# One change to a fused language-model layer: where chunk 15's output product, chunk 1's taps and the experts' casts stand

## The chip, the cores and the metric

The kernel runs on one core of one Trainium2 chip. The core has TensorE (matrix products, which write to PSUM), VectorE, ScalarE and GpSimd for everything else, and SyncE, which only starts transfers here. The engines run side by side, each through its own stream of instructions in order, and wait for one another on semaphores. The metric is the device time of one launch in microseconds (us), smaller being better.

## The reference

The reference computes one layer of a language model on 2 x 2048 tokens of width 192:

- a token embedding (a table of 70 rows, scaled) plus a sine position code;
- a Mamba-2 mixer on the normed stream: an input projection to `z`, `x`, `B`, `C` and `dt`; a causal convolution with 4 taps and a SiLU; a state recurrence for 24 heads of 16 channels with 64 states, `h = exp(dt*A) h + dt x B`, `y = h C + D x`; a gate `y * silu(z)`; an output projection; then an RMS norm and a gated MLP of width 768;
- a mixture of experts: a sigmoid router that picks 2 of 8 experts from 2 of 4 groups, gated experts of width 128, and one shared expert of the same shape.

```
h = tok(x)
h = h + attn(layernorm(h))      # mixer, then + m = MLP(rmsnorm(mixer))
h = h + ffn(layernorm(h))       # sum of two chosen experts + the shared one
```

## The kernel before

**Tiling.** The 2048 positions are cut into 16 chunks of 128 positions (`NC`, `Q`), both batch entries (`NB` = 2) side by side. The recurrence runs in chunked form. Within a chunk, pairwise decays are exponentials of differences of running sums, which a transfer through DRAM (`sums_in_rows`, tile `ri`) and a matrix product (`exponents`, line 1707) lay out, ScalarE exponentiates (`exponentials`, line 782, tile `er`) and VectorE cuts and multiplies (`masks`, line 1193, tile `mr`); `masked` (line 1718) sums them on TensorE into the bank `p_y`. There are 12 such units a chunk (`NR`), 6 for each batch entry. What comes from earlier chunks is read out of a state (`state_read`, line 1809; `from_state`, line 1204), and the state is decayed by GpSimd (`decayed`) and added to (`state_share`, line 1818; `new_state`, line 1219). `skipped_x` (line 1795) adds `D x`; `scanned` (line 1213) makes `y`, GpSimd's `gate` (line 510) multiplies it by `silu(z)`, and `project_out` (line 1831) is the output product, with 3 matrix products for each batch entry.

**Stages.** Each chunk has a pre part (embedding, norm), a front part (projection, convolution, scan operands), a scan, and a back part (output product, RMS norm, MLP called `swiglu`, second norm, router, experts). `run` calls `ramp`, then `body(2, 1, 0)`, which is the first round, then a hardware loop of 13 rounds `body(i+2, i+1, i)`, then `finale(14, 15)`. A round interleaves the pre and front part of one chunk, the scan of the next and the back part of the oldest. In the finale both last chunks are left: the scan of chunk 15 beside the back part of 14, and then, interleaved, the experts of 14 and the back part of 15.

**What sets the order.** No planner: every engine has its own `ramp`, `body` and `finale`, and the order of calls in it is the order in its stream. Waits are written out (`wait_ge` on a semaphore that counts chunks or units).

**PSUM.** There are 8 banks: `p_pair[0..1]`, `p_out[0..1]`, `p_misc`, `p_d0`, `p_d1`, `p_y`. Exponents alternate between `p_d0` and `p_d1`. In the finale, the gate and up products of chunk 14's experts go to the banks that `p_gu_a` lists, and chunk 15's output product goes to `p_misc`, both batch entries in a row, behind `gate_up(1)`; ScalarE's `mixed` and `mixed_norm` and VectorE's `v_low` and `mixed` read it there.

**The weights.** High parts in 16 bit are cast from the 32-bit weights, low parts are the rest. The input columns are done first; the middle ones (`middle_weights`, 1536 columns; high on ScalarE, low on VectorE, line 1049) in the ramp; the experts' ones (`last_weights`, 2312 columns) have their high part cast by GpSimd (line 590) at the end of the ramp, and their low part made by VectorE in four halves (line 1057) within the first `swiglu`.

**The convolution.** ScalarE copies the projected `x` out of PSUM (`convolved_in`) and does the first tap (`first_tap`); VectorE adds the three other taps for each of four groups of channels (`taps(c, m)`, line 1132, three instructions each); ScalarE's `convolved_first` (line 707) and `convolved_rest` (line 716) apply the SiLU and write `xs`, and wait until all the readers of the chunk before are through.

**The pair sums.** `operands` writes the running sums into `lj`, first the high part on ScalarE (line 749), then the low part on VectorE (line 1169), and SyncE sends them.

## Time and profile before

| | us |
|---|---|
| median of 3 runs | 796.21 |
| lowest, highest | 795.14, 796.4 |
| the profiled execution | 796.69 |
| its span, first to last instruction | 794.9 |
| TensorE busy | 757.6 (95%) |
| VectorE busy | 636.5 (80%) |
| ScalarE busy | 546.8 (69%) |
| GpSimd busy | 328.3 (41%) |

The profile is of one execution. A share of busy time is a mean over stages with different limits, so a change in one stage is read from the waits and windows of that stage. The profile's clock column (PEclk) gives the TensorE clock that was granted, as a share of 2.4 GHz.

### The profile page before, as it was taken

To read this page: it belongs to the slowest core of one execution; us is meant where nothing else is said; L and a number is where in the kernel's file an instruction comes from. 1 tells how busy PE (TensorE), PEld (TensorE's weight loads), DVE (VectorE), ACT (ScalarE), POOL (GpSimd) and SP (SyncE) were. 2 spreads that over 40 slices of the span, in tenths; PEclk is the share of its full clock that TensorE was granted. 3 is DMA by queue.
4 is the path that set the end of the run, shared out by engine and by line. 5 is a ranking of instruction groups with operands and counts; after the bars stand their busy time and mean duration, and the time that the engine had idled before them with its cause. 6 is when DMAs were issued, how large, how long until landed. Compare 5 with 4: busy or idle time off the path is not lost.

```text
span 794.9 us, 23059 instructions
## 1 busy us (share of the span) xinstructions
PE 757.6 (95%) x7278; PEld 646.6 (81%) x7278; DVE 636.5 (80%) x1691; ACT 546.8 (69%) x1242; POOL 328.3 (41%) x478
## 2 busy tenths in 40 slices
PE   2679999999999999999999999999999999999897
PEld 1556788988888898888888888888988888888786
DVE  4699987879788787978878797887889788786745
ACT  4975777767777776777767677776767777675533
POOL 5355544433444443344344334434443443442222
PEclk9899999999999999999999999999999999999999
DMA  7420000000000000000000000000000000000000
GB/s 251 155 89 1 12 22 12 9 25 6 15 10 21 10 6 25 3 17 10 21 10 6 25 3 17 10 21 10 6 24 4 17 10 16 14 6 11 2 1 21
DMA packets 14923, 18.93 MB, mean 24 GB/s; under 512 B 4656, under 2 KB 13008, under 8 KB 14448
## 3 DMA queue, kind: packets, MB, share of 16 engines
q1 hardware_dynamic: 13264, 15.25, 6.0%
q0 software_dynamic: 1632, 3.34, 1.7%
q8 instruction: 15, 0.25, 0.1%
q14 instruction: 12, 0.10, 0.0%
HBM read 14.39 MB, written 4.19 MB: 23 GB/s over the span
## 4 chain that ended last, share of the span: by engine, by line
PE 87%; DVE 2%; issue 1%; ACT 1%; POOL 0%; DVEq 0%; POOLq 0%; ACTq 0%
PE bank L1554 40%; PE bank L1934 11%; PE bank L1862 8%; PE bank L1718 6%; PE bank L1707 5%; PE bank L1831 4%; PE bank L1818 3%; PE bank L1809 3%; PE bank L1795 2%; PE bank L1647 1%; PE bank L1652 1%; PE bank L1691 1%; DVE mr L1193 1%; PE bank L1901 0%; PE bank L1902 0%
## 5 line engine op out<-in xcount | busy, mean ns | idle before, releaser
L1193 DVE SCALAR_TENSOR_TENSOR mr<-er,gm 128x512 f32<-128x512 f32 x192 | 125.8, 692 | 4.1 <-ACT er L782 3.7
L782 ACT ACTIVATE er<-bank 128x512 f32<-128x512 f32 x192 | 106.0, 595 | 27.4 <-PE bank L1707 27.1
L1934 PE MATMUL bank<-w2t,w_raw 128*128 128x192 f32 x576 | 112.6, 327 | 0.4 <-DVE w_raw L1362 0.4
L872 ACT ACTIVATE sg<-bank 128x256 f32<-128x256 f32 x144 | 55.1, 382 | 61.8 <-PE bank L1554 50.9
L1132 DVE SCALAR_TENSOR_TENSOR xa<-xr,cw_,xa 128x256 f32<-128x256 f32 x192 | 92.4, 488 | 6.3 <-ACT xa L690 4.7
L1934 PEld LDWEIGHTS bank<-w2t,w_raw 128*128 128x128 f32 x576 | 91.0, 190 | 1.8 <-DVE w_raw L1455 0.7
L1554 PE MATMUL bank<-x_h,wt_lo 128*128 128x256 f16 x288 | 78.5, 273 | 0.0
L1554 PE MATMUL bank<-x_h,w_lo 128*128 128x256 f16 x288 | 78.5, 273 | 0.0
L1554 PE MATMUL bank<-x_l,w_hi 128*128 128x256 f16 x288 | 78.5, 272 | 0.0
L1554 PE MATMUL bank<-x_h,w_hi 128*128 128x256 f16 x288 | 78.4, 272 | 0.0
L1554 PE MATMUL bank<-x_h,wt_hi 128*128 128x256 f16 x288 | 78.4, 272 | 0.0
L1862 PE MATMUL bank<-wd,gt 128*128 128x192 f32 x384 | 74.3, 329 | 1.4 <-DVE gt L1239 1.4
L566 POOL TENSOR_TENSOR w_raw<-w_raw 128x384 f32<-128x384 f32 x64 | 64.0, 1000 | 14.9 <-ACT w_raw L860 8.7
L821 ACT ACTIVATE sg<-bank 128x256 f32<-128x256 f32 x90 | 33.9, 376 | 51.5 <-PE bank L1554 51.5
L1362 DVE TENSOR_TENSOR w_raw<-sg,bank 128x256 f32<-128x256 f32 x144 | 59.9, 416 | 11.7 <-ACT sg L872 10.8
L1707 PE MATMUL bank<-ri,lj 128*128 128x512 f16 x192 | 63.7, 384 | 3.3 <-DMA ri<-sums 1.8
L1862 PEld LDWEIGHTS bank<-wd,gt 128*128 128x128 f32 x384 | 60.9, 190 | 2.6 <-DVE gt L1239 2.0
L1718 PE MATMUL bank<-mr,xd 128*32 128x128 f32 x1536 | 57.0, 283 | 1.6 <-DVE mr L1193 1.6
L503 POOL TENSOR_TENSOR state<-state,ends 128x384 f32<-128x384 f32 x31 | 31.8, 1027 | 64.1 <-PE bank L1569 38.3
L1455 DVE SCALAR_TENSOR_TENSOR w_raw<-bank,cw,w_raw 128x192 f32<-128x192 f32 x128 | 47.5, 413 | 10.4 <-POOL w_raw L566 7.5
L445 POOL TENSOR_SCALAR var<-mv 128x2 f32<-128x2 f32 x32 | 7.2, 225 | 113.1 <-DVE mv L1270 62.7
L1239 DVE TENSOR_TENSOR gt<-sg,bank 128x256 f32<-128x256 f32 x90 | 36.2, 414 | 21.9 <-ACT sg L821 21.9
(239 smaller groups left out, 2197.3 us busy)
## 6 DMA issues: line engine op xcount, KB each, us to landing
out<-w_raw SPq DMA_DIRECT2D x16, 192.0 KB, 2.0
pos<-position SPq DMA_DIRECT2D x16, 96.0 KB, 1.9
ri<-exponent_rows SPq DMA_DIRECT2D x1, 1536.0 KB, 6.4
w_raw<-weights SPq DMA_DIRECT2D x1, 1156.0 KB, 6.0
wt_raw<-weights SPq DMA_DIRECT2D x1, 1156.0 KB, 8.4
sums<-lj SPq DMA_DIRECT2D x16, 64.0 KB, 1.9
w2t<-w SPq DMA_DIRECT2D x1, 864.0 KB, 11.6
w_raw<-weights SPq DMA_DIRECT2D x1, 768.0 KB, 8.1
```

Source lines behind the costliest of these rows:

```text
L566: pool.tensor_tensor(acc[:], acc[:], wt_out[:, e % NWT], ALU.add).then_inc(acc_done, 1)
L782: act.activation(er[:, r % NER], p_d[r % 2][:].rearrange("p (h i) -> p h i", h=HG), ACT.Exp)\
L872: act.activation(sg[:, e % 4, :], src[e][:, 0:NB * Q], ACT.Silu).then_inc(sx_ready, 1)
L1132: ve.scalar_tensor_tensor(xa[:, m], xr[:, m, :, k:k + Q], cw_[:, m, k:k + 1], xa[:, m], ALU.mult, ALU.add)\
L1193: ve.scalar_tensor_tensor(mr[:, r % NMR], er[:, r % NER], 1.0, gm[:, r // NQ, :].unsqueeze(1).to_broadcast([128, HG, Q]), ALU.min, ALU.mult)\
L1362: ve.tensor_tensor(hh[:, e % NHH, :], sg[:, e % 4, :], src[e][:, NB * Q:2 * NB * Q], ALU.mult)\
L1455: ins = ve.scalar_tensor_tensor(acc[:, b], p_ex[e][:, b * D:(b + 1) * D], cw[:, b, e - 1:e], acc[:, b], ALU.mult, ALU.add)
L1554: ins = pe.matmul(out_, a, b, start=(i == 0), stop=(i == len(parts) - 1))
L1707: pe.matmul(p_d[r % 2][:].rearrange("p (h i) -> p h i", h=HG), lj[:, b, f, :], ri[:, of, b, f, :], start=True, stop=True).then_inc(d_done, 1)
L1718: ins = pe.matmul(p_y[row:row + 32, k * Q:(k + 1) * Q], xd[:, b, h, :], mr[:, r % NMR, heads.index(h), :], start=False, stop=(h % 2 == 1), ...
L1862: ins = pe.matmul(dst[:, b * D:(b + 1) * D], gt[:, f, b * Q:(b + 1) * Q], wd[:, f, :], start=(f == 0 and b == 0), stop=(f == NF - 1), skip ...
L1934: ins = pe.matmul(p_ex[e][:, b * D:(b + 1) * D], hh[:, e % NHH, b * Q:(b + 1) * Q], w2t[:, e, :], start=True, stop=True)
```

## The change

The names and semaphores:

- `xs_skipped` is a new semaphore, raised by the last `skipped_x` of a chunk. `convolved_first` and `convolved_rest` wait for it and no longer for the last masked product (`yq_done`). So that it comes early, `second_scan` (called in the ramp) issues its three `skipped_x` together.
- Finale: `project_out(15, 0)` is issued ahead of `turn_x(14)`, `project_out(15, 1)` stays behind `gate_up(1)`. Both go to `p_d1`; `gate_up(3)` goes to `p_misc`. `project_out(15, 0)` waits for all of chunk 15's exponentials, `gate_up(3)` for `t1_ready[1]`, `mlp(1)` also for `hm_ready`.
- Ramp: chunk 1's taps stand one place earlier each in VectorE's stream; `operands(0)` goes ahead of `gates(0, 0)` on ScalarE and ahead of `taps(0, 3)` on VectorE; the first middle weights on ScalarE come behind the first four exponentials and `first_tap(1, 1)`.
- GpSimd's two casts of the experts' high parts leave the end of the ramp and stand in the first round, one behind `mixed(0)`, one behind `gate(1, 0)`.

```diff
--- before.py
+++ after.py
@@ -286,7 +286,7 @@
         m_ready = sem("m_ready")
-        yq_done = sem("yq_done")
+        yq_done, xs_skipped = sem("yq_done"), sem("xs_skipped")
         xw_ready = [sem(f"xw_ready{b}") for b in range(NB)]
@@ -310,7 +310,7 @@
         p_gu = (p_pair[0], p_pair[1], p_d0, p_d1, p_pair[0], p_pair[1], p_y, p_pair[1], p_pair[0])
-        p_gu_a = (p_pair[0], p_pair[1], p_d0, p_d1, p_pair[0], p_pair[1], p_pair[0], p_pair[1], p_pair[0])
+        p_gu_a = (p_pair[0], p_pair[1], p_d0, p_misc, p_pair[0], p_pair[1], p_pair[0], p_pair[1], p_pair[0])
         before_a = (None, None, None, None, 0, 1, 4, 5, 6)
@@ -613,19 +613,21 @@
                 halo(1)
-                last_weights(w_hi, w_raw)
-                last_weights(wt_hi, wt_raw)
 
             def body(p, f, b):
...
                 mixed(b)
+                if not later(b):
+                    last_weights(w_hi, w_raw)
                 if f is not None:
...
                     gate(f, 0)
+                if not later(b):
+                    last_weights(wt_hi, wt_raw)
                 if p is not None:
@@ -703,7 +705,7 @@
                     act.wait_ge(xt_done[1], c)
-                    act.wait_ge(yq_done, c * NR)
+                    act.wait_ge(xs_skipped, c)
                 act.activation(xs[:, 0:2], xa[:, 0:2], ACT.Silu).then_inc(xs_first, 1)
...
             def convolved_rest(c):
@@ -712,7 +714,7 @@
                     act.wait_ge(yi_done[1], c)
-                    act.wait_ge(yq_done, c * NR)
+                    act.wait_ge(xs_skipped, c)
                 act.activation(xs[:, 2:NM], xa[:, 2:NM], ACT.Silu).then_inc(xs_ready, 1)
@@ -915,9 +917,9 @@
                 expert_gate(a, 1, p_gu_a)
-                mixed(b, p_misc)
+                mixed(b, p_d1)
                 expert_gate(a, 2, p_gu_a)
-                mixed_norm(b, p_misc)
+                mixed_norm(b, p_d1)
                 expert_gate(a, 3, p_gu_a)
@@ -959,8 +961,8 @@
                 gates(0, 1)
+                operands(0, p_pair[1])
                 gates(0, 0)
-                operands(0, p_pair[1])
                 convolved_first(0)
@@ -971,10 +973,10 @@
                 on_channels(0)
-                middle_weights(0)
                 exponentials(0, range(4))
...
                 first_tap(1, 1)
+                middle_weights(0)
                 exponentials(0, (4, 5))
@@ -1418,10 +1420,10 @@
                 route_experts(a, None, p_gu_a)
-                v_low(b, p_misc)
+                v_low(b, p_d1)
                 route_weights(a, p_gu_a)
                 hidden(a, 4, p_gu_a)
-                mixed(b, p_misc)
+                mixed(b, p_d1)
                 low_in(b, vl_turned, p_d0[:, 0:NB * Q], v_l, v_lo_ready)
@@ -1483,28 +1485,28 @@
                 pre_split(1, p_pair[0][:, NB * Q:2 * NB * Q])
-                taps(0, 3)
                 ve.wait_ge(setup_p, SETUP_P)
                 operands(0, p_pair[1])
+                taps(0, 3)
                 steps_dt(1, p_pair[0])
...
                 masked_g(0)
+                taps(1, 0)
                 masks(0, range(4))
                 from_state(0, 0)
-                taps(1, 0)
+                taps(1, 1)
                 masks(0, (4, 5))
-                taps(1, 1)
                 new_state(0, 0)
                 scanned(0, 0)
+                taps(1, 2)
                 masks(0, (6, 7))
-                taps(1, 2)
+                taps(1, 3)
                 masks(0, (8, 9))
...
                 scanned(0, 1)
-                taps(1, 3)
                 new_state(0, 1)
@@ -1744,7 +1746,8 @@
             def second_scan(c, p, turn, sums=None):
...
                 pe.wait_ge(y_sum[0], c + 1)
-                skipped_x(1, 0)
+                for k in range(KT):
+                    skipped_x(1, k)
                 masked(c, (6, 7))
@@ -1753,12 +1756,10 @@
                     sums()
-                skipped_x(1, 1)
                 masked(c, (8, 9))
...
                     project_in_x(p, p_d, (2, 3), c)
-                skipped_x(1, 2)
                 masked(c, (10, 11))
...
             def scan_front(c, turned):
@@ -1792,8 +1793,10 @@
             def skipped_x(b, k):
-                pe.matmul(p_y[:, k * Q:(k + 1) * Q], skip[:, k], xs[:, k, b, :], start=(k == 0), stop=False,
-                          skip_group_check=True)
+                ins = pe.matmul(p_y[:, k * Q:(k + 1) * Q], skip[:, k], xs[:, k, b, :], start=(k == 0), stop=False,
+                                skip_group_check=True)
+                if b == NB - 1 and k == KT - 1:
+                    ins.then_inc(xs_skipped, 1)
 
             def state_read(c, b, p):
@@ -1818,8 +1821,8 @@
             def project_out(c, b, dst=p_out[0]):
-                if b == 0 and dst is p_misc:
-                    pe.wait_ge(t1_ready[1], c + 1)
+                if b == 0 and dst is p_d1:
+                    pe.wait_ge(e_ready, c * NR + NR)
                 elif b == 0:
@@ -1985,11 +1988,18 @@
                 swiglu(a, None, b)
-                scan_back(b, None, lambda: turn_x(a, None))
+
+                def turn_beside_output():
+                    project_out(b, 0, p_d1)
+                    turn_x(a, None)
+
+                scan_back(b, None, turn_beside_output)
 
                 def gate_up(e):
...
                         pe.wait_ge(gt_ready, a * NF + NF - 1 + e)
+                    elif e == 3:
+                        pe.wait_ge(t1_ready[1], b + 1)
                     elif before_a[e] is None:
@@ -1999,6 +2009,8 @@
                 def mlp(f):
...
                         pe.wait_ge(hh_ready, a * NX + 3 + f)
+                        if f == 1:
+                            pe.wait_ge(hm_ready, b + 1)
                     else:
@@ -2006,8 +2018,7 @@
                 gate_up(1)
-                project_out(b, 0, p_misc)
-                project_out(b, 1, p_misc)
+                project_out(b, 1, p_d1)
                 gate_up(2)
```

## Rows read from the trace of the kernel before

**Rows 1.** The page, part 4: shares of the chain by engine.

```profile
PE 87%; DVE 2%; issue 1%; ACT 1%; POOL 0%; DVEq 0%; POOLq 0%; ACTq 0%
```

**Rows 2.** Windows by stage: us, busy us (and count) by engine, PEclk, DMA share, GB/s.

```profile
62.00:84.00 22.00, 19.95 (x180) 15.29 (x178) 20.50 (x37) 12.86 (x29) 11.86 (x11) 1.00 0.02 5
...
84.00:735.00 651.00, 650.41 (x6364) 560.65 (x6361) 539.14 (x1461) 467.70 (x1073) 271.35 (x401) 1.00 0.05 13
...
735.00:743.00 8.00, 5.97 (x69) 4.49 (x68) 5.88 (x14) 4.63 (x9) 1.49 (x2) 0.79 0.01 3
```

**Rows 3.** What TensorE waited for, 70 to 84 us: us, times, longest.

```profile
PE bank L1862 <- DVE gt L1239: 1.4, 2, 1.1
```

**Rows 4.** Timeline of TensorE, finale: start, us, engine, line, operation [idle before].

```profile
739.43 0.33 PE L1901 MATMUL bank<-idf,xn 128*128 128x128 f32 x1 [1.99 <-DVE xn L1281]
...
740.34 2.79 PE L1718 MATMUL bank<-mr,xd 128*32 128x128 f32 x48
...
745.51 2.12 PE L1831 MATMUL bank<-wo,y 128*128 128x192 f32 x12
```

**Rows 5.** Timelines of ScalarE, GpSimd and VectorE, finale.

```profile
735.24 2.23 ACT L782 ACTIVATE er<-bank 128x512 f32<-128x512 f32 x4
...
725.93 1.00 POOL L510 TENSOR_TENSOR y<-y,zs 128x384 f32<-128x384 f32 x1 [0.63 <-DVE y L1213]
...
741.77 0.42 DVE L1065 TENSOR_TENSOR x_h<-bank,x_h 64x256 f16<-64x256 f32 x1
```

**Rows 6.** Window of 1 us, columns as in rows 2.

```profile
740.00:741.00 1.00, 1.00 (x17) 0.62 (x19) 1.00 (x3) 0.53 (x2) 0.00 (x0) 0.50 0.00 0
```

**Rows 7.** Chain of waits, last loop round: start, us, what.

```profile
694.24 1.47 PE bank L1718 x48
```

**Rows 8.** Timeline of GpSimd, end of the ramp and first round.

```profile
53.75 1.16 POOL L510 TENSOR_TENSOR y<-y,zs 128x384 f32<-128x384 f32 x1 [3.76 <-DVE y L1213]
...
58.10 2.11 POOL L590 CAST wt_hi<-wt_raw 128x2312 f16<-128x2312 f32 x1
...
64.79 1.17 POOL L516 TENSOR_TENSOR rm<-vv,mhalf 128x2 f32<-128x2 f32 x1
...
71.72 1.00 POOL L510 TENSOR_TENSOR y<-y,zs 128x384 f32<-128x384 f32 x1 [0.63 <-DVE y L1213]
```

**Rows 9.** Timeline of TensorE, ramp.

```profile
34.37 0.60 PE L1707 MATMUL bank<-ri,lj 128*128 128x512 f16 x2 [1.79 <-DMA ri<-sums]
...
56.70 1.25 PE L1647 MATMUL bank<-idf,xs 128*128 128x128 f32 x6 [3.84 <-issue]
```

**Rows 10.** Timeline of VectorE, ramp and first round.

```profile
26.19 1.51 DVE L1132 SCALAR_TENSOR_TENSOR xa<-xr,cw_,xa 128x256 f32<-128x256 f32 x3
...
53.59 2.13 DVE L1132 SCALAR_TENSOR_TENSOR xa<-xr,cw_,xa 128x256 f32<-128x256 f32 x3
...
57.35 1.20 DVE L1180 TENSOR_TENSOR xd<-bank,dt_ 128x384 f32<-128x384 f32 x2 [1.04 <-PE bank L1647]
...
58.47 3.35 DVE L1049 SCALAR_TENSOR_TENSOR w_lo<-w_raw,nrm,w_hi 128x1536 f16<-128x1536 f32 x1
...
64.05 3.73 DVE L1193 SCALAR_TENSOR_TENSOR mr<-er,gm 128x512 f32<-128x512 f32 x5
...
72.78 0.42 DVE L1239 TENSOR_TENSOR gt<-sg,bank 128x256 f32<-128x256 f32 x1 [1.14 <-ACT sg L821]
...
73.72 1.35 DVE L1057 TENSOR_TENSOR w_lo<-w_raw,w_hi 128x1156 f16<-128x1156 f32 x1
```

**Rows 11.** Timeline of ScalarE, end of the ramp.

```profile
55.75 0.63 ACT L716 ACTIVATE xs<-xa 128x512 f32<-128x512 f32 x1 [2.11 <-DVE xa L1132]
...
59.43 0.26 ACT L762 ACTIVATE ends<-bank 128x96 f32<-128x96 f32 x1
```

**Rows 12.** GpSimd's line 492: count, ns min/median/max, first and last start.

```profile
L492 POOL TENSOR_TENSOR xw<-xd,ends x31: 837/842/2351, 31.6 to 715.8; 128x384 f32<-128x384 f32 x31
```

**Rows 13.** VectorE's line 1193, columns as in rows 12.

```profile
L1193 DVE SCALAR_TENSOR_TENSOR mr<-er,gm x192: 674/684/1327, 35.4 to 740.2; 128x512 f32<-128x512 f32 x192
```

## The prediction

> **What bounds the kernel now.** Read the chain of waits first: TensorE carries 87% of it [rows 1]. Then the windows of the stages [rows 2]: between 84 and 735 us TensorE is busy for 650.41 of 651 us. The steady loop is therefore TensorE's own work, and the change must pay elsewhere. It touches three places: the ramp (0 to 62 us), the first round, in which chunk 0's back part runs beside chunk 1's scan (62 to 84 us, VectorE busy for 20.50 of 22 us), and the joint between the last two back parts (735 to 743 us, TensorE busy for 5.97 of 8 us at a granted clock of 0.79). In the first round TensorE waits for VectorE's gated products `gt` twice, 1.4 us in all [rows 3]: there VectorE sets the end.
>
> **The loop.** TensorE issues the same instructions in the same order, `second_scan` being called in the ramp alone. `convolved_first` and `convolved_rest` wait on `xs_skipped` in place of `yq_done`, which both come before. One semaphore increment a chunk is added. Cost 0, because a loop without idle time shows no wait that could go; a bound from both sides is 0.1 us.
>
> **The finale: last chunk's output product.** `project_out(15, 0)` is half of 12 records that take 2.12 us [rows 4], so 1.0 us. It moves from behind `gate_up(1)` to ahead of `turn_x(14)`. Its operands are there: ScalarE's last four exponentials end at 735.24 + 2.23 = 737.47 us, the gate product of batch 0 at 726.93 us [rows 5]. TensorE stands idle for 1.99 us until the transposes of `xn` start at 739.43 us [rows 4], so the product ends at 738.5 us, 0.9 us before anybody wants its engine. Gain 1.0 us, if what follows moves up too. It does: `m_out` comes 1.0 us earlier, and the chain from it (squares, `rm` on GpSimd, `v_t`, `v_low`) is followed by work in VectorE's order, so the later wait of TensorE for the low part moves with it and doesn't grow. The new bank of `gate_up(3)` waits only for `t1_ready[1]`, and `mlp(1)` for `hm_ready`, both long past by the order of the streams.
>
> The second part is the clock. After the 1.99 us of idle the granted clock is 0.50 (1.2 GHz) in 740 to 741 us, and the 48 masked products take 2.79 us, where in the loop the same 48 take 1.47 us [rows 4, 6, 7]. With a product in the gap 0.9 us of idle is left, and I expect 2.4 GHz. Of the 1.3 us VectorE lets through only a part: the router waits for the low part `x_h`, which ends at 742.19 us [rows 5] and which VectorE's masks set, not TensorE. The router starts behind the masked products at 743.1 us, so at most 0.9 us; I take 0.8. The bounds are 0 (the clock falls all the same) and 0.9. Finale: 1.0 + 0.8 = 1.8 us.
>
> **The ramp, before Y.** Call Y the end of `scanned(0, 1)`; it is now at 53.7 us, where GpSimd's gate product starts [rows 8]. At the front, ScalarE and VectorE do chunk 0's pair sums before its last taps, so the transfer of the sums, for which TensorE waits 1.79 us until 34.37 us [rows 9], starts some 1.1 us earlier. But the taps (3 in 1.51 us [rows 10]) end 1.2 us later, and with them the SiLU, the transposes and the exponentials on channels. ScalarE drops the first middle weights ahead of the exponentials and does them after `first_tap(1, 1)`. Together the first exponent leaves at about 34.05, not 34.37 us: gain 0.3 us, bounds -0.5 and +0.8, because one side is a DMA that I cannot time under the other's load. From there to Y VectorE has no gap now, and its work up to Y grows by chunk 1's fourth group of taps: +1.5 us. `taps(1, 0)` goes into the wait for the first exponentials, but then `new_state(0, 0)` has to wait for TensorE's state product, which takes that gain back: each later group has only taken the place of the one before. Y = 53.7 - 0.3 + 1.5 = 54.9 us.
>
> **The ramp, after Y.** Now the three taps stand behind Y (53.59 us, 2.13 us), `convolved_rest(1)` waits 2.11 us for them, and TensorE idles 3.84 us until 56.70 us [rows 9 to 11]. All this goes: the transposes start at Y + 0.1 = 55.0 us, 1.7 us earlier. The next to come late is ScalarE: `gates(1, ...)` waits for GpSimd's gate product (1.1 to 1.2 us after Y [rows 8]), then come its gates, a table load and the copy of `bt`, which from the end of `xs` (56.38) to that of the `ends` (59.69 us) take 3.3 us now, about 0.5 of it for `bc`, which will be done before [rows 11]: 54.9 + 1.1 + 2.7 = 58.7 us, 1.0 us earlier. VectorE's `w_lo` now takes 3.35 us, because GpSimd's second cast runs until 60.21 us [rows 8, 10]; 1156 columns of the like take 1.35 us [rows 10], so its 1536 want 1.7 to 1.8. `masked_g` follows at 58.6 us, then GpSimd's first `weighted_x` (0.84 us [rows 12]), `wt_lo` (1.7 us), the second `weighted_x` (0.84 us), one behind the other, and the first mask of chunk 1. It ends at about 62.8, against 65.4 us now (64.05 and the longest mask, 1.33 us [rows 10, 13]): gain 2.6 us, Y's own delay counted.
>
> **The casts in the first round.** Each is 2.11 us on GpSimd [rows 8]. GpSimd has room for both; the price falls on VectorE. The row is `w_lo`: started at 58.47 us beside a cast with 1.74 us to go, it took 1.6 us more than its columns want. `xw` takes 2351 ns at most against 842 in the middle, a mask 1327 against 684 [rows 12, 13]. So I let an instruction of VectorE that reads two SBUF operands stand still while GpSimd casts, and one with an operand in PSUM run: two `xd` took 1.20 us beside the casts [rows 10]. The Trainium skill has the same in "SBUF — State Buffer", section "Who interferes with whom": a VectorE instruction with two SBUF inputs contends with a GpSimd one that reads SBUF, and the loser is blocked for the whole of the other. That rule speaks against this change, and the trace agrees with it (3.35 us).
>
> The first cast now follows `rm`, which ends at 65.96 us, 6.3 us after the `ends`, 0.4 of it for the second `weighted_x` [rows 8, 11]; changed, 58.7 + 5.9 = 64.6 us. VectorE is then in chunk 1's masks (0.64 us each, two SBUF operands). The cast comes either ahead of mask 4, and costs the whole 2.1 us, or behind it, when `from_state` and `v_low`, with one operand in PSUM each, run beside it, and costs 1.1 us. Mask 4 would start at 62.8 + 3 x 0.64 = 64.7 us, 0.1 us from the cast; I take the middle, 1.6 us. The second cast follows `gate(1, 0)`. Now VectorE's first `w_lo` half of the experts ends at 75.0 us, 2.3 us behind that gate's end at 72.72 us [rows 8, 10]. With 2.11 us of cast between gate and one of mask 6 and `w_lo`, it comes 2.11 + 0.64 + 1.27 = 4.0 us behind it: costs 1.8 us. From there to 84 us VectorE is dense, so nothing of it is made up. Bounds of both casts together: 0 and 4.2 us, with 3.4 taken, near the upper end because the nearest row, `w_lo`, shows the whole overlap as lost.
>
> **The sum.** Ramp and first round: -2.6 + 1.6 + 1.8 = +0.8 us. Finale: -1.8 us. Together -1.0 us. The profiled execution took 796.69 us (span 794.9 and 1.8 around it), so it would take 795.7. The runs' median is 796.21, half a microsecond shorter; the clock's fall in the finale may be a part of that and is then gained in some executions only, so I take 0.8 off the median: 795.4 us.
>
> **Rivals.** First, the casts are hidden after all: the first comes behind mask 4 and the second falls beside `gt` products, of which one operand is in PSUM. Then the sum is -1.8 - 2.6 + 1.1 = -3.3 us, some 793 us; with half of that hidden, -2.2 us. For it: VectorE waits 1.1 us for ScalarE just there [rows 10]. Against it: GpSimd's gate fills that wait already. Chance 0.36 for all that ends more than 1.6 us below. Second, on the other side: TensorE's clock falls in the waits that the change opens. One is new at 29 us (about 0.8 us, for the late taps), another grows in the first round from 1.4 us by the 1.8 us of the second cast. The price of one fall is the finale's, 2.79 - 1.47 = 1.3 us, or up to 1.5 us where more dense work follows; both give +3.0, in sum +2.0 us, 798.2 us. It decides once it costs over 1.0 us, two falls or one that hits dense work; against it, a wait of 1.1 us in the first round now leaves the clock at 1.00 [rows 2, 3]. Chance 0.12 for more than 1.6 us above. Third, the change doesn't do what it says: the product in the finale waits longer than the gap lasts and pushes the transposes. Then the finale gives 0 to 1.0 us and the time is 796.2 to 797; its operands' ends [rows 5] speak against it, and it counts with my forecast's own band, 0.05.
>
> **Numbers.** My forecast, no change that can be told, has 0.52 with the third rival in it; faster 0.36, slower 0.12. A measurement of this kernel tells about 0.2%, 1.6 us, from no change. The range goes from 793.1 (casts hidden) to 797.3 us (one fall of the clock beside the upper costs).
>
> **What would show it.** Right: the output product's 6 records before the `xn` transposes and no 0.50 in the clock around 740 us; the wait before chunk 1's transposes down from 3.84 us to under 1.5; `w_lo` of the middle weights near 1.7 us; one mask of chunk 1 and mask 6 or the first `w_lo` of the experts longer by up to 2 us beside a cast; the loop's length the same to 0.3 us. Wrong: masks at 0.68 us beside the casts (then the first rival), Y below 54 us, or the end of the first round more than 1 us away from +0.8.

## The result, and the profile after

The changed kernel takes 797.29 us (median of 20 runs, 795.37 to 799.14), the kernel before 796.1 us in the same comparison (20 runs, 794.39 to 796.91): ratio 1.0016, 95% interval 1.0010 to 1.0023. It is slower by 1.2 us: 0.16%, inside the 0.2% that the text called no change, but the interval leaves no change out. 795.4 us was forecast. The time lies at the edge of the range (797.3), and the sign is wrong. Four of the 20 runs took 795.37 to 795.75 us, about the forecast's time; of none of them is there a trace. The profiled execution took 797.69 us with a span of 795.9, against 796.69 and 794.9 before, so the two traces differ by the same 1.0 us as is to be explained.

The first view is the windows of the stages of the changed kernel (us, busy us and count by engine, granted clock, DMA share, GB/s); they answer to [rows 2]. In this kernel lines up to 1,100 have moved by 2, those behind by 2 or 3.

```profile
62.00:84.00 22.00, 19.41 (x166) 14.56 (x164) 18.15 (x31) 10.39 (x26) 10.45 (x10) 0.90 0.01 1
84.00:735.00 651.00, 649.34 (x6353) 559.68 (x6353) 541.19 (x1464) 468.57 (x1074) 273.52 (x402) 1.00 0.05 13
735.00:743.00 8.00, 7.21 (x58) 6.00 (x60) 4.78 (x13) 4.06 (x7) 1.49 (x2) 1.00 0.00 1
```

The joint in the finale is as forecast: TensorE busy for 7.21 us in place of 5.97, clock 1.00 in place of 0.79. The first round is not: VectorE, which set the end there, is busy for 18.15 us in place of 20.50, and the clock is 0.90.

The residual sum `h` closes each chunk, so its rows cut the span into stages. VectorE's timeline of `h`, the kernel before, chunks 0, 14 and 15:

```profile
84.24 0.55 DVE L1257 TENSOR_TENSOR h<-bank,hm 128x384 f32<-128x384 f32 x1
...
735.50 0.56 DVE L1257 TENSOR_TENSOR h<-bank,hm 128x384 f32<-128x384 f32 x1 [1.12 <-PE bank L1862]
...
767.67 0.56 DVE L1257 TENSOR_TENSOR h<-bank,hm 128x384 f32<-128x384 f32 x1 [0.56 <-PE bank L1862]
```

The same rows of the changed kernel:

```profile
87.04 0.55 DVE L1259 TENSOR_TENSOR h<-bank,hm 128x384 f32<-128x384 f32 x1
...
738.08 0.56 DVE L1259 TENSOR_TENSOR h<-bank,hm 128x384 f32<-128x384 f32 x1 [1.12 <-PE bank L1865]
...
768.68 0.56 DVE L1259 TENSOR_TENSOR h<-bank,hm 128x384 f32<-128x384 f32 x1 [0.56 <-PE bank L1865]
```

Ramp and first round lost 2.80 us (87.04 - 84.24), the loop gained 0.22 (651.04 against 651.26), the finale gained 1.57 (30.60 against 32.17), and behind the last `h` both take 27.2 us: 2.80 - 0.22 - 1.57 = 1.01 us. The finale was forecast at -1.8, the loop at 0; ramp and first round at +0.8. There lies the miss of 2.0 us.

VectorE's timeline of the changed kernel from Y on (start, us, engine, line, operation, [idle before <- releaser]); it answers to [rows 10]:

```profile
54.23 0.56 DVE L1215 TENSOR_TENSOR y<-bank,t 128x384 f32<-128x384 f32 x1
...
56.39 1.81 DVE L1051 SCALAR_TENSOR_TENSOR w_lo<-w_raw,nrm,w_hi 128x1536 f16<-128x1536 f32 x1
...
58.88 2.31 DVE L1051 SCALAR_TENSOR_TENSOR wt_lo<-wt_raw,nrm,wt_hi 128x1536 f16<-128x1536 f32 x1
61.11 1.92 DVE L1195 SCALAR_TENSOR_TENSOR mr<-er,gm 128x512 f32<-128x512 f32 x2
63.50 0.69 DVE L1195 SCALAR_TENSOR_TENSOR mr<-er,gm 128x512 f32<-128x512 f32 x1 [0.47 <-ACT er L784]
65.39 3.21 DVE L1195 SCALAR_TENSOR_TENSOR mr<-er,gm 128x512 f32<-128x512 f32 x2 [1.19 <-ACT er L784]
68.52 0.54 DVE L1206 TENSOR_TENSOR t<-bank,ecx 128x384 f32<-128x384 f32 x1
...
74.28 0.42 DVE L1241 TENSOR_TENSOR gt<-sg,bank 128x256 f32<-128x256 f32 x1 [1.36 <-ACT sg L823]
74.61 1.98 DVE L1195 SCALAR_TENSOR_TENSOR mr<-er,gm 128x512 f32<-128x512 f32 x1
76.52 1.35 DVE L1059 TENSOR_TENSOR w_lo<-w_raw,w_hi 128x1156 f16<-128x1156 f32 x1
```

TensorE in the same stretch, in answer to [rows 9]:

```profile
54.89 0.85 PE L1649 MATMUL bank<-idf,xs 128*128 128x128 f32 x6 [1.08 <-DVE y L1215]
...
59.45 1.03 PE L1709 MATMUL bank<-ri,lj 128*128 128x512 f16 x2 [2.14 <-DMA ri<-sums]
60.28 2.13 PE L1834 MATMUL bank<-wo,y 128*128 128x192 f32 x6
```

TensorE of the kernel before, the same instructions:

```profile
60.65 0.59 PE L1707 MATMUL bank<-ri,lj 128*128 128x512 f16 x2 [0.57 <-ACT ecx L770]
61.08 1.14 PE L1831 MATMUL bank<-wo,y 128*128 128x192 f32 x6
```

And GpSimd of the changed kernel, in answer to [rows 8]:

```profile
58.74 3.15 POOL L492 TENSOR_TENSOR xw<-xd,ends 128x384 f32<-128x384 f32 x2 [2.71 <-ACT ends L764]
...
65.74 2.31 POOL L590 CAST w_hi<-w_raw 128x2312 f16<-128x2312 f32 x1
...
73.94 2.11 POOL L590 CAST wt_hi<-wt_raw 128x2312 f16<-128x2312 f32 x1
```

Y ends at 54.8 us (54.9 forecast). The 3.84 us wait before chunk 1's transposes is 1.08, and `w_lo` takes 1.81 us in place of 3.35. The masks start at 61.11 us, 2.94 us earlier than before. Up to here the steps held. Then comes what the sum has no term for: VectorE waits 0.47 and 1.19 us for ScalarE's exponentials `er`. TensorE's first two exponents start only 1.20 us earlier than before (59.45 against 60.65). It waited 2.14 us for the transferred pair sums of chunk 1 (before, 0.57 us in this place, and for ScalarE's `ecx`), and then did chunk 0's output product at 1.2 GHz: 2.13 us for six products, against 1.14 before. The fall of the clock is not new but has moved: before, it came behind the wait of 3.84 us, the granted clock was 0.50 in 58 to 60 us and 0.90 in 60 to 62; now it is 0.85 and then 0.50. The first cast stands beside the fifth mask (the pair takes 3.21 us, unhindered 1.29), the second beside the seventh (1.98 against 0.69).

From before to after, VectorE's path to `w_lo` of the experts moves by: masks' start -2.94; waits for `er` +1.66; the five masks' own time +2.09 (5.82 against 3.73); between `t` and the first `gt` +0.69; the seventh mask +1.30. Of the 2.09 us, 1.92 are the held pair's. That is +2.80 us, and `w_lo` starts at 76.52 in place of 73.72 us.

### The profile page after: what moved, and what is told of

It reads as the page before. It is cut to its first block, busy times and chain, and to the rows that moved or that the text cites. A ratio compares the mean times of both kernels' runs of the same rounds, so it can differ in the third digit from the quotient of the medians.

```text
span 795.9 us, 23060 instructions
## 1 busy us (share of the span) xinstructions
PE 755.6 (95%) x7278; PEld 644.3 (81%) x7278; DVE 638.4 (80%) x1691; ACT 546.5 (69%) x1242; POOL 325.8 (41%) x478
## 4 chain that ended last, share of the span: by engine, by line
PE 89%; DVE 4%; issue 3%; ACT 1%; DMA 1%; POOL 1%; DVEq 0%; POOLq 0%; SPq 0%; ACTq 0%
PE bank L1556 40%; PE bank L1937 11%; PE bank L1865 8%; PE bank L1720 6%; PE bank L1709 5%; PE bank L1834 4%; PE bank L1821 3%; PE bank L1812 3%; PE bank L1796 2%; PE bank L1649 1%; DVE mr L1195 1%; PE bank L1654 1%; PE bank L1693 1%; DVE xa L1134 1%; PE bank L1904 0%
## 5 line engine op out<-in xcount | busy, mean ns | idle before, releaser
L1195 DVE SCALAR_TENSOR_TENSOR mr<-er,gm 128x512 f32<-128x512 f32 x192 | 129.2, 709 | 2.0 <-ACT er L784 1.7
L1720 PE MATMUL bank<-mr,xd 128*32 128x128 f32 x1536 | 55.0, 278 | 1.4 <-DVE mr L1195 1.4
L1556 PE MATMUL bank<-v_h,w_hi 128*128 128x256 f16 x192 | 52.6, 274 | 0.8 <-issue 0.8
```

The lines of the kernel that those rows point to most:

```text
L1195: ve.scalar_tensor_tensor(mr[:, r % NMR], er[:, r % NER], 1.0, gm[:, r // NQ, :].unsqueeze(1).to_broadcast([128, HG, Q]), ALU.min, ALU.mult)\
L1556: ins = pe.matmul(out_, a, b, start=(i == 0), stop=(i == len(parts) - 1))
L1720: ins = pe.matmul(p_y[row:row + 32, k * Q:(k + 1) * Q], xd[:, b, h, :], mr[:, r % NMR, heads.index(h), :], start=False, stop=(h % 2 == 1), ...
```

## The experiments

Two theories. **C**: the casts, where they now are, hold VectorE's instructions with two SBUF operands, and that is the loss. **K**: the loss is TensorE's, which waits for the transferred sums and falls to 1.2 GHz. All kernels were timed against the kernel before; h(0) and h(15) are the starts of `h` of chunks 0 and 15 in the profiled execution, in us. They tell of one execution each, which can lie 2 us off its kernel's median. The kernel before ran beside each group again, with medians of 795.79 to 796.08 us, so kernels of different groups are compared by the ratio.

| kernel | median (lowest to highest) | ratio, 95% interval | h(0) | h(15) |
|---|---|---|---|---|
| before | 796.1 | | 84.24 | 767.67 |
| changed | 797.29 (795.37-799.14) | 1.0016, 1.0010-1.0023 | 87.04 | 768.68 |
| e1 finale alone | 794.8 (793.6-795.28) | 0.998, 0.9972-0.9989 | 84.05 | 765.75 |
| e2 casts alone | 797.59 (795.59-799.57) | 1.002, 1.0009-1.0031 | 87.56 | 770.26 |
| e3 changed, both casts back | 794.79 (794.57-795.16) | 0.9987, 0.9979-0.9996 | 84.27 | 765.92 |
| e4 ramp's order alone | 796.04 (795.57-797.53) | 1.0004, 0.9995-1.0013 | 84.18 | 767.40 |
| e5 casts on ScalarE | 795.95 (794.41-796.61) | 0.9996, 0.9988-1.0005 | 83.68 | 766.76 |
| e6 e5 + early sums | 795.9 (794.39-797.09) | 1.0001, 0.9992-1.001 | 82.77 | 765.80 |
| e7 e6 + filler | 795.09 (794.66-796.26) | 0.9994, 0.9985-1.0002 | 83.18 | 766.28 |
| e8 changed + early sums, filler | 794.77 (794.52-798.65) | 1.0008, 0.9994-1.0021 | 83.96 | 765.58 |
| e9 first cast back | 795.48 (794.27-796.61) | 0.9996, 0.9987-1.0005 | 84.11 | 765.86 |
| e10 second cast back | 796.16 (794.66-797.44) | 1.0003, 0.9994-1.0012 | 85.45 | 767.30 |
| e11 e8, second cast back | 796.11 (795.34-797.38) | 1.0002, 0.9993-1.0011 | 85.52 | 767.32 |
| e12 e3 + two tiny ScalarE copies | 794.99 (794.53-796.61) | 0.9991, 0.9982-1.0 | 83.86 | 765.59 |
| e13 casts placed | 795.41 (793.56-798.74) | 1.0001, 0.9987-1.0015 | 83.08 | 765.65 |
| e14 e13 + early sums | 795.7 (794.15-796.38) | 0.9994, 0.9985-1.0003 | 82.99 | 765.39 |
| e15 e14 + filler | 794.79 (793.87-796.29) | 0.999, 0.9982-0.9999 | 84.78 | 767.28 |

### The three parts by themselves

**e1**, the finale's edits on the kernel before:

```
-        p_gu_a = (p_pair[0], p_pair[1], p_d0, p_d1,
+        p_gu_a = (p_pair[0], p_pair[1], p_d0, p_misc,
...
+                def turn_beside_output():
+                    project_out(b, 0, p_d1)
+                    turn_x(a, None)
```

> The kernel before with the finale's part of the change alone (output product of batch 0 of chunk 15 beside the wait for xn, banks exchanged). In the traces the finale, from the sum h1 of chunk 14 on, is 1.6 us shorter after the change. If that gain is the output product's own (1.0 us) and the clock's (0.6 us), it stands alone: 794.5 us, ratio 0.998. Rival: part of it was only lent by the ramp (the clock's phase shifts with everything ahead), then 1.0 us alone: 795.1 us.

The finale's own time is 30.60 us (765.75 - 735.15), as in the changed kernel: 1.57 us gained. By the ratio it is faster. This part does what was forecast.

**e2**, the two casts moved on the kernel before, all else as it was:

```
                 mixed(b)
+                if not later(b):
+                    last_weights(w_hi, w_raw)
...
                     gate(f, 0)
+                if not later(b):
+                    last_weights(wt_hi, wt_raw)
```

> The kernel before with GpSimd's two casts moved into the first round and nothing else. Theory C (a cast blocks VectorE's two-operand instructions wherever it stands): the ramp's w_lo falls from 3.35 to 1.8 us, so the first mask of chunk 1 comes about 1.6 us earlier; then one mask is 2 us longer beside the first cast and mask 6 or the experts' w_lo 1.3 to 1.8 us longer beside the second. In sum +1.5 to +2 us: 797.6 to 798.1 us. Theory K (the wait for the transferred sums and TensorE's clock took the time, the casts are the smaller part): +0.5 us or less.

h(0) is 3.32 us later than before, in an execution that was the longest of its twelve (799.57 us, 2.0 above the median); 0.64 us of it is there at the start of `y` already. VectorE's timeline of this kernel:

```profile
59.37 1.81 DVE L1051 SCALAR_TENSOR_TENSOR w_lo<-w_raw,nrm,w_hi 128x1536 f16<-128x1536 f32 x1
...
66.39 3.21 DVE L1195 SCALAR_TENSOR_TENSOR mr<-er,gm 128x512 f32<-128x512 f32 x2 [0.45 <-ACT er L784]
...
74.93 2.19 DVE L1195 SCALAR_TENSOR_TENSOR mr<-er,gm 128x512 f32<-128x512 f32 x1
```

`w_lo` is relieved by 1.5 us, and the masks pay 1.9 and 1.5. The casts alone make the kernel slower, without the ramp's new order.

**e3**, the changed kernel with both casts back behind `halo(1)` in the ramp (the reverse of the diff above):

> The kernel after with the two casts put back to the end of the ramp, all else as after. Theory C: the casts now hold up both w_lo and wt_lo of the middle weights (they stand just before them, about 2 + 2 us, partly beside VectorE's waits), but the masks of the first round run free; time 795.3 us, about 2 us below after. Theory K: the wait for ri (2.1 us) and the output product at 1.2 GHz stay as they are, so the first round stays late: 796.8 to 797.3 us, no more than 0.5 us below after.

VectorE in the ramp of this kernel:

```profile
56.64 3.29 DVE L1049 SCALAR_TENSOR_TENSOR w_lo<-w_raw,nrm,w_hi 128x1536 f16<-128x1536 f32 x1
...
60.19 3.32 DVE L1049 SCALAR_TENSOR_TENSOR wt_lo<-wt_raw,nrm,wt_hi 128x1536 f16<-128x1536 f32 x1
63.43 4.37 DVE L1193 SCALAR_TENSOR_TENSOR mr<-er,gm 128x512 f32<-128x512 f32 x5
```

Both low parts are held here (3.29 and 3.32 us, against 1.81 and 2.31), h(0) is 84.27 as before, and the time is e1's. So the ramp's new order is worth nothing, although it brings chunk 1's transposes from 56.70 to 55.15 us. The casts, which now fall beside both low parts, take most of it; the masks start 0.62 us earlier than before (64.05) and then take 0.64 us more (3.73), two of them 1.32 us each in place of one, beside GpSimd's second `xw`, which the casts have pushed back.

**e4**, the ramp's orders and `xs_skipped` alone on the kernel before:

> The kernel before with the ramp's orders and the xs_skipped waits alone (taps and pair sums one place forward, skipped_x together), casts at the end of the ramp, finale as before. It should be e3 plus the finale's gain: e3 + 1.6 us. Theory C: 796.9 us (about +0.8 against before). Theory K: 798.4 to 798.9 us. If the three parts add up, e1 + e4 differences equal e3's within 0.5 us.

No change, h(0) 84.18.

### Casts off GpSimd, and TensorE's wait

**e5**, the changed kernel with the casts on ScalarE, behind `convolved_rest(1)` and behind `mixed_norm(0)`:

```
+            def last_weights(hi, raw):
+                x = slice(COL_E, COLS)
+                act.wait_ge(in_experts, 32)
+                act.copy(hi[:, x], raw[:, x]).then_inc(w_last_hi, 1)
```

> The kernel after with the two casts done by ScalarE (the first behind convolved_rest(1), the second behind mixed_norm(0)) and none by GpSimd. Theory C (GpSimd's casts block VectorE; e2 and e3 price them at 1.5 and 2.5 us): no mask or w_lo longer than about 1.9 us, the same casts cost next to nothing on an engine that shares nothing with VectorE: 794.3 us, at or below e3. Rival (it is the place and the length of the casts, not the engine: whatever stands there delays the round): ScalarE is on the way to the gates and to v_h, so 796 to 797 us.

The casts take 2.12 and 2.13 us there, and no mask is held by one. TensorE waits 2.43 us for the sums all the same. h(0) is 83.68: 3.36 us of the changed kernel's h(0) come from GpSimd's casts together with what they delay. (The median falls by less, since this kernel's loop is 1.4 us longer, of which more below.)

**e6** sends the sums earlier: VectorE does chunk 1's pair sums ahead of chunk 0's last two masks.

```
                 from_state(0, 1)
-                masks(0, (10, 11))
                 operands(1, p_out[0])
+                masks(0, (10, 11))
```

> As e5, and on VectorE the low pair sums of chunk 1 (operands(1)) ahead of masks(0, (10, 11)). Theory K (with the casts away, the rest of the ramp's gain is held back by TensorE's wait for the transferred sums, 2.1 us in the trace of after): the transfer starts 1.3 us earlier, the wait falls under 1 us, time e5 - 0.5 to - 1.0 us. Rival (VectorE or ScalarE bounds there anyway): same as e5 within 0.3 us.

TensorE waits almost as long, now for ScalarE:

```profile
59.80 0.59 PE L1713 MATMUL bank<-ri,lj 128*128 128x512 f16 x2 [1.97 <-ACT ecx L768]
```

The exponents start 0.74 us behind the start of `ecx`, in e5 0.98, in the changed kernel 0.90. So the transfer came last there, but only by about 0.2 us: the wait itself is ScalarE's as much. What differs is the clock. It did not fall in this execution: the output product takes 1.14 us in place of 2.03, the five masks run without a gap from 61.62 us, and h(0) is 82.77, 0.91 us less than e5's. The medians, 795.95 and 795.9, show nothing of it.

**e7** adds nine filler products of 512 columns on TensorE behind `sums_on_channels(1)`, of which the result is not used:

> As e6, with 9 matrix products of 512 columns into the unused bank p_out[1] behind sums_on_channels(1), about 2 us of work in TensorE's wait, which change no result. Theory K with the clock: exponents, output products and turns of the first round run at 2.4 GHz (the output product 1.1 us for a batch entry, not 2.1), time e6 - 0.5 to - 1.0 us. Rival (the clock is hidden behind VectorE): same as e6; if the filler holds up the first exponents, +0.3 us.

h(0) is 83.18. As the clock had not fallen in e6's profiled execution either, this doesn't tell what the filler is worth. The medians are lower with it, 795.09 against 795.9 here and 794.79 against 795.7 for e15 and e14 below, but the intervals of the ratios overlap: a gain is possible and not shown.

**e8**, early sums and filler on the changed kernel, casts on GpSimd in the first round:

> The kernel after, casts on GpSimd in the first round as they are, with e6's early pair sums and e7's filler. It tells how much of the missing time is the wait and the clock. Theory K: the first masks keep the 2.6 us that the sum gave them, and the time falls by 1.5 to 1.9 us to 795.5 us. Theory C: the casts still block 2.1 and 1.3 us; earlier masks meet the first cast in the same place, so no more than 0.7 us: 796.6 us.

The profiled execution was one of the short ones (794.6 us). VectorE there (the fifth of the masks starts at 64.81):

```profile
61.74 3.75 DVE L1195 SCALAR_TENSOR_TENSOR mr<-er,gm 128x512 f32<-128x512 f32 x5
65.41 0.55 DVE L1206 TENSOR_TENSOR t<-bank,ecx 128x384 f32<-128x384 f32 x1
65.88 0.75 DVE L1073 SCALAR_TENSOR_TENSOR v_t<-bank,rm,v_t 128x192 f16<-128x192 f32 x2
66.53 1.48 DVE L1195 SCALAR_TENSOR_TENSOR mr<-er,gm 128x512 f32<-128x512 f32 x1
...
71.54 3.26 DVE L1059 TENSOR_TENSOR w_lo<-w_raw,w_hi 128x1156 f16<-128x1156 f32 x1
```

and GpSimd:

```profile
64.83 2.63 POOL L590 CAST w_hi<-w_raw 128x2312 f16<-128x2312 f32 x1
...
71.01 2.57 POOL L590 CAST wt_hi<-wt_raw 128x2312 f16<-128x2312 f32 x1
```

The cast was issued at 64.83 us, 0.02 behind the fifth mask's start; it waited that mask out (2.63 us in place of 2.11) and then lay beside `t` and `v_t`, which read a bank and kept their 0.55 and 0.75 us; the sixth mask paid 0.8 us. The second cast held `w_lo` for 1.9. Seven runs took 794.5 to 794.8 us, five 797 to 798.7; that in the latter the cast came ahead of the fifth mask is likely, but no trace of one was taken. The ratio takes in both groups, so it is above 1 with a median of 794.77.

### Each cast's price

**e9**, only the first cast back in the ramp:

> The changed kernel, with only the first of the two high casts (w_hi) put back behind GpSimd's halo(1) in the ramp; the second stays in the first round. Theory C (each cast that lies beside VectorE's masks in the round costs its own block): mask 4 is no longer blocked for 1.9 us, and in the ramp the cast's block on w_lo (1.81 to about 3.3 us) is hidden by TensorE's wait for the transferred sums; the second cast still blocks mask 6 by 1.3. h of chunk 0 at about 85.1 (87.04 in the changed kernel, 84.27 with both back), median about 795.5. Theory K (the round is late because TensorE waits for the sums and runs at 1.2 GHz, whatever GpSimd does): h at about 87.0, median 797.3. A third reading, that the two casts cost only together since one pushes the other, gives h near 84.3 and 794.8.

**e10**, only the second one back:

> The changed kernel, with only the second cast (wt_hi) put back into the ramp; the first stays behind mixed(b) in the first round. Theory C: mask 4 stays blocked (about 2 us), mask 6 is 0.69 instead of 1.98, the ramp's wt_lo is 3.3 instead of 2.31 and that is hidden by the wait for the sums. h of chunk 0 at about 85.7 and a median of about 796.1; the two single prices (1.9 + 1.3) should add up to the 2.8 to 3.2 that both cost. Theory K: 87.0 and 797.3. Together only: 84.3 and 794.8.

| h(0) | second cast in the ramp | second in the round |
|---|---|---|
| first cast in the ramp | 84.27 (e3) | 84.11 (e9) |
| first in the round | 85.45 (e10) | 87.04 (changed) |

In these four executions moving the second cast costs -0.16 us while the first is in the ramp, and +1.59 behind a moved first one; moving the first costs 1.18 or 2.93. But in e9's the clock did not fall behind the wait for the sums, in the other three it did (rows in the last section). By the medians the second cast's move costs 0.69 or 1.13 us, the first's 1.37 or 1.81. The two ways differ by 0.44 us, and the runs (11 to 20 of each kernel) are spread over 0.6 to 3.8 us: that the prices don't add is not shown. In e9 the second cast holds the seventh mask (2.19 us in place of 0.69), but the masks start 1.0 us earlier than in e3 (62.41 against 63.43), because the ramp holds one cast less: the same time at another place. With both moved the masks find no `er`. Between e10 and the changed kernel, whose clocks both fell, they come 0.80 us nearer to the start of `y` (6.88 us behind it in place of 7.68) and wait 0.65 us longer (1.66 against 1.01): most of what leaving the ramp gives is lost in a wait, and the round still pays for both.

**e11**, e8 with the second cast back in the ramp:

> The changed kernel with the early pair sums and the nine filler products (as in the run with both before), and the second cast put back into the ramp. There the first cast cost only 0.8 us (mask 5) and the second 1.9 (w_lo). Theory C: in the ramp the second cast blocks wt_lo by about 1.0 (3.3 instead of 2.31) and is not hidden, since TensorE no longer waits for the sums; net gain about 0.9: h of chunk 0 at about 83.1 (83.96 with both in the round), median about 794.0, the fastest of all. Rival: in the ramp the cast waits for GpSimd's xw and pushes the products into ends and the first mask (1 to 2 us): h 84 or later, median 794.8 or more.

The expectation failed: h(0) 85.52 in place of 83.1. The ramp's part came as expected (masks from 62.51 us), but the cast was issued at 65.60 us, 0.17 ahead of the fifth mask, while the fourth ran:

```profile
65.16 0.69 DVE L1194 SCALAR_TENSOR_TENSOR mr<-er,gm 128x512 f32<-128x512 f32 x1
...
65.77 2.60 DVE L1194 SCALAR_TENSOR_TENSOR mr<-er,gm 128x512 f32<-128x512 f32 x1
```

It got in between the two and held the fifth for its whole length. The same first cast cost 0.8 us in e8 and 1.9 here.

**e13** fixes the slots. The first cast waits for the fifth mask; the second stands behind `decayed(1, 0)`:

```
                 mixed(b)
                 if not later(b):
+                    pool.wait_ge(m_ready, NR + NQ - 1)
                     last_weights(w_hi, w_raw)
                 if f is not None:
                     pool.wait_ge(vl_turned, b + 1)
                     decayed(f, 0)
+                if not later(b):
+                    last_weights(wt_hi, wt_raw)
```

> The changed kernel, both casts still on GpSimd in the first round, but placed: the first waits for chunk 1's fifth mask, so that it lies beside t (0.55 us) and v_t (0.75), which read a bank; the second stands right behind decayed(1,0), beside hm, state, y and the wait for sg, which read banks too, instead of behind gate(1,0). Theory S (only VectorE's instructions with two SBUF operands are held): the fifth mask takes its 0.68 instead of 2.6, the sixth about 1.5 instead of 0.68, the seventh 0.69 instead of 1.98; h of chunk 0 falls from 87.04 to about 84.7, median about 795.2. Rival W (a cast costs the round its 2.1 us wherever it lies, by GpSimd's own queue or by holding every VectorE instruction): h stays within 0.5 of 87.0 and the median at 797; t, v_t, hm or y would show 2 us in place of 0.55.

VectorE of this kernel:

```profile
64.56 1.29 DVE L1197 SCALAR_TENSOR_TENSOR mr<-er,gm 128x512 f32<-128x512 f32 x2 [0.29 <-ACT er L786]
65.77 0.55 DVE L1208 TENSOR_TENSOR t<-bank,ecx 128x384 f32<-128x384 f32 x1
66.24 0.75 DVE L1075 SCALAR_TENSOR_TENSOR v_t<-bank,rm,v_t 128x192 f16<-128x192 f32 x2
66.89 1.69 DVE L1197 SCALAR_TENSOR_TENSOR mr<-er,gm 128x512 f32<-128x512 f32 x1
...
69.40 0.56 DVE L1223 TENSOR_TENSOR state<-state,bank 64x384 f32<-64x384 f32 x1
69.99 0.56 DVE L1217 TENSOR_TENSOR y<-bank,t 128x384 f32<-128x384 f32 x1
70.85 0.42 DVE L1243 TENSOR_TENSOR gt<-sg,bank 128x256 f32<-128x256 f32 x1 [0.30 <-ACT sg L825]
71.19 0.69 DVE L1197 SCALAR_TENSOR_TENSOR mr<-er,gm 128x512 f32<-128x512 f32 x1
```

and GpSimd:

```profile
65.92 2.11 POOL L590 CAST w_hi<-w_raw 128x2312 f16<-128x2312 f32 x1 [0.97 <-DVE mr L1197]
67.99 1.28 POOL L503 TENSOR_TENSOR state<-state,ends 128x384 f32<-128x384 f32 x1
69.22 2.10 POOL L590 CAST wt_hi<-wt_raw 128x2312 f16<-128x2312 f32 x1
```

Two casts of 2.11 and 2.10 us in the same round, and beside them `t`, `v_t`, `state` and `y` keep their times. They cost 1.0 us at the sixth mask, and 0.8 us behind the seventh, where GpSimd's copy of `h` and gate, which now come later, stand beside `w_lo` (1.66 us in place of 1.35) and `h_next` (1.02 in place of 0.55). h(0) falls by 3.96 us to 83.08, more than expected, since in this execution the clock did not fall behind TensorE's 2.32 us wait for the sums: VectorE waits 0.29 us for `er` in place of 1.66. The median, 795.41, came as expected (795.2); by the ratios, 1.0001 against 1.0016, it is below the changed kernel's. What a cast costs is set by the VectorE instructions beside it.

**e14** and **e15** add the early sums, and the early sums and the filler:

> As the run with placed casts, and VectorE's pair sums ahead of the last two masks of chunk 0, so that TensorE's wait for the transferred sums goes. Theory S: masks of chunk 1 from about 61.6 without a wait, t at about 65.4, gt near 70.5, w_lo near 71.5 at 1.35 us; h of chunk 0 at about 82.5 and a median of about 793.2, below every kernel so far. Rival W: h 84.5 or later, 795 or more.

> As the run before it, with the nine filler products of 512 columns that keep TensorE's clock up in the ramp. With theory S and the casts out of the way, h of chunk 0 at about 82.2 (the run with the casts on ScalarE, early sums and filler had 83.18, without the filler 82.77, so the filler may bring nothing or cost 0.4): 82.2 to 82.9, median 792.9 to 793.6. If TensorE's clock were what bounds this stretch, it would be at least 1 us below the run without the filler.

h(0) is 82.99 in e14, 0.5 us short of the expectation, and the median 795.7 in place of 793.2. e15's profiled execution was late in the ramp (clock 0.991, masks only from 63.02 us), its median 794.79. Neither beats e1 or e3.

### Where an earlier first round went

e6 has h(0) 1.28 us ahead of e1's, and h(15) 0.05 us behind. From e6's fourth chunk on, each takes 46.63 to 46.67 us from `h` to `h`, where before, e1 and e3 take 46.54 to 46.59; from h(0) to h(14) e6 takes 1.33 us more than e1. e5, e7, e13, e14 and e15 have it too, e8 to e11 do not. One round of before and of e6, laid side by side, keep one lasting step apart: the output product starts 0.51 us behind the start of the two exponents ahead of it in the former, 0.60 in the latter. **e12** asked whether two more instructions in ScalarE's stream are enough:

```
                 convolved_rest(1)
+                act.copy(warm[:, 1:2], mhalf[:, 0:1])
```

> The kernel with the casts in the ramp (finale and ramp parts only), with two one-column copies added on ScalarE at the two places where the casts stood in the ScalarE runs (behind convolved_rest(1), and behind mixed_norm(0)). In those runs a chunk took 46.64 us from h to h instead of 46.56, some 1.1 us over the loop, which ate what their earlier first round had brought. If two further instructions in ScalarE's stream are enough for it (where the stream's code lies), the pitch is 46.64 here too, last h about 1.1 us later than 765.92 and the median about 795.9. If it is the casts' own work, or that ScalarE writes the high halves, the pitch stays 46.56 and the median 794.8.

They are not: its rounds take 46.54 to 46.58 us. The cause of the longer round stays open.

## Why the prediction was wrong, step by step

**The failed step** is "It ends at about 62.8, against 65.4 us now [...]: gain 2.6 us, Y's own delay counted." The end itself was right (about 62.4 us), but it went into the sum as if VectorE stayed the bound after it. The masks read ScalarE's exponentials, and these follow TensorE's exponents, which hang on the transfer of chunk 1's pair sums (VectorE makes them only at 53.36 us), on `ecx`, and on an output product ahead of the third. The text itself had ScalarE's `ends` only 1.0 us earlier and the masks 2.6, and did not lay the chain from the one to the other: measured, the exponents came 1.20 us earlier and the masks 2.94, and VectorE waited 1.66 us. Most of that is the clock: in e13, whose wait for the sums is 2.32 us but whose clock stayed at 2.4 GHz, VectorE waits 0.29 us.

The other term at nothing is the 0.69 us between `t` and `gt`. The held fifth mask keeps `t` back, TensorE waits 1.85 us for it and then runs at a granted clock of 0.66 in 69 to 74 us. In e2 the same wait left the clock at 1.00, and from `t` to `gt` it took 5.07 us as before, against 5.76 in the changed kernel. TensorE there, the changed kernel and then e2:

```profile
69.16 1.16 PE L1821 MATMUL bank<-xw,bt 128*128 128x384 f32 x2 [1.85 <-issue]
```

```profile
70.17 0.88 PE L1820 MATMUL bank<-xw,bt 128*128 128x384 f32 x2 [1.85 <-issue]
```

With the masks' start 0.34 us better than forecast, 1.66 + 0.69 - 0.34 is 2.0 us, the miss in the profiled execution. Both theories hold a part: the casts cost 3.2 us and led to the second fall of the clock; behind the wait for the sums it was the first fall that cost time, more than the wait.

**The casts.** 1.6 and 1.8 us were taken. In the changed kernel the pair with the held fifth mask took 1.92 us more and the seventh 1.30, so 3.2 us together, nearly as forecast. (From its own rows the second price was 1.7: 4.0 less the 2.35 us between 72.72 and 75.07.) The mechanism held as well: e13 shows both sides of it. The Trainium skill's "SBUF — State Buffer", section "Who interferes with whom", had the rule, and the traces agree: 3.26 us for a `w_lo` of 1.35 beside a cast, 0.55 for `t` beside one.

**The sum of the two.** Leaving the ramp gives something only if the masks then find their `er`, and between e10 and the changed kernel 0.65 of 0.80 us were lost in that wait. A term by term sum of -2.6, +1.6 and +1.8 hid that the first term was the casts' own relief: with the casts left in the ramp the new order is worth 0 (medians: e3 794.79 against e1's 794.8, e4 796.04 against 796.08 before).

**The rivals.** The second one, a fall of TensorE's clock in waits that the change opens, was given 0.12 and 798.2 us. It is what the profile shows, at other places than named: in the wait for the sums at 59 us, and in the 1.85 us at 67.3 to 69.2 us while VectorE's held mask kept `t` back. The other 19 runs have no trace, so how often the clock fell is not known. The first rival (casts hidden) is refuted by e2 and by the changed kernel's own masks. The third did not come: the product ended ahead of the transposes.

**The finale.** 1.57 of 1.8 us, and the clock 1.00 as expected. **The loop:** 0.22 us shorter, within the ±0.3 that the text allowed though outside its bound of 0.1. **Ramp before Y:** right at 54.8, with a wait of 1.44 us for the state product at 43.73 us where it was named. The first exponent left at 34.63, not 34.05 us: the transfer's wait was gone, but ScalarE's `ecx` was now the late one (0.99 us); it cost nothing at Y.

## What to carry to other kernels

A copy on GpSimd is not priced by its length but by what VectorE runs beside it: put it beside instructions that read a bank, and pin it there with a wait: issued 0.02 us behind a mask's start it cost 0.8 us, 0.17 us ahead of one 1.9. When a stall goes, list for each engine the input that its next instructions wait for, transfers too, before the gain is carried on. Where a chain on another engine moves by less than yours, the difference is a wait. Time a change's parts separately: here the finale alone is worth 0.2%, and the casts took that and more. And read what one execution says against the median of many before two prices are compared.

## What the runs showed of the hardware

GpSimd and VectorE took turns. A cast issued during a mask waited for that mask alone (2.63 us in place of 2.11 in e8), went ahead of the next one although VectorE had it ready, and held it for its whole length (2.60 us in place of 0.69 in e11).

TensorE's clock did not fall each time behind an equal wait. Timelines of TensorE behind its wait for the sums, e9 and then e10:

```profile
59.96 0.61 PE L1708 MATMUL bank<-ri,lj 128*128 128x512 f16 x2 [2.15 <-DMA ri<-sums]
60.40 1.14 PE L1833 MATMUL bank<-wo,y 128*128 128x192 f32 x6
```

```profile
59.13 0.79 PE L1708 MATMUL bank<-ri,lj 128*128 128x512 f16 x2 [2.12 <-DMA ri<-sums]
59.72 2.13 PE L1833 MATMUL bank<-wo,y 128*128 128x192 f32 x6
```

After 2.15 us of idle the six products take 1.14 us (2.4 GHz), after 2.12 us they take 2.13 (1.2 GHz). e13 (2.32 us of idle, 1.14) and e3 (2.44 us, 2.13) are such a pair too, and so are e2 and the changed kernel behind their 1.85 us. That may be why runs of one kernel scatter: e13's three longest, 798.12 to 798.74 us, have a mean clock of 0.989, its four shortest, 793.56 to 794.42, 0.996 to 0.998.

A wait that the profile calls "issue" can hide a real one: TensorE's 1.85 us before `xw,bt` at 69.16 us in the changed kernel ends 0.10 us behind VectorE's `t`, as in e9 and e10 (0.10 and 0.09), where `t` ends at 66.61 and 68.79 us.
